# One chunk in twelve units gathered by SyncE with byte offsets, edge attributes issued by ScalarE, node updates inside the convolution's loop

## The reference, cut to what matters

```python
# attention: for each of three edge types t, over the edges of that type
xw = x @ W[t]; e = leaky_relu(a_s[src] + a_d[dst]); w = exp(e - max over dst)
out += segment_sum(w * xw[src]) / segment_sum(w) + bias[t]
# convolution
filters = silu(edge_attr @ fW1 + fb1) @ fW2 + fb2
messages = (x[src] @ dW + db) * filters
agg = segment_sum(messages, dst)
x + silu(agg @ uW1 + ub1) @ uW2 + ub2        # the node update
```

## Time and profile before

| | us |
|---|---|
| median of 3 runs | 4148.93 (4147.18 to 4151.31) |
| span of the profiled execution, which is its own time as far as it is given | 4155.8 |
| TensorE busy | 3395.1 |
| GpSimd busy | 3070.8 |
| VectorE busy | 2388.6 |
| ScalarE busy | 1364.7 |
| share of the 16 DMA engines: GpSimd's queue, SyncE's queue | 19.6%, 6.1% |

### The profile page before, as it was taken

One profiled execution on the slowest core, in us unless ns is written; L12 is line 12 of the kernel. 1 busy time (PEld: TensorE's weight loads), 2 busy tenths in 40 slices (PEclk: granted clock), 3 DMA queues, 4 the chain that ended last, 5 costly groups with the idle time before them and its releaser, 6 DMA issues.

```text
span 4155.8 us, 58597 instructions
## 1 busy us (share of the span) xinstructions
PE 3395.1 (82%) x13945; PEld 2624.2 (63%) x13946; DVE 2388.6 (57%) x5253; ACT 1364.7 (33%) x3361; POOL 3070.8 (74%) x3239
## 2 busy tenths in 40 slices
PE   5788788888888888888777888888888888788888
PEld 3566666666666666666555666666666666667666
DVE  7888888888888888888842322322332323223223
ACT  5455555555555555555411111111111111111111
POOL 5777777777777777777657777777777777777775
PEclk7555555555555555555577666676666666766667
DMA  4222222222222222222223222222222222222222
GB/s 124 56 59 61 59 59 61 60 59 61 59 59 61 59 59 61 59 59 61 58 60 98 77 74 76 71 76 75 71 76 73 74 75 72 75 76 71 76 74 79
DMA packets 180619, 286.01 MB, mean 69 GB/s; under 512 B 82273, under 2 KB 123054, under 8 KB 176011
## 3 DMA queue, kind: packets, MB, share of 16 engines
q0 software_dynamic: 102656, 213.73, 19.6%
q1 hardware_dynamic: 77856, 71.32, 6.1%
HBM read 271.06 MB, written 12.49 MB: 68 GB/s over the span
## 4 chain that ended last, share of the span: by engine, by line
POOL 36%; issue 12%; POOLq 1%; PE 1%; DMA 0%; DVE 0%; DVEq 0%
POOL ce_xg L63 36%; POOLq L676 0%; PE ce_ring L1429 0%; PE ce_ps_h L1420 0%; PE ce_ring L1420 0%; POOLq L677 0%; PE ce_ps_h L1407 0%; POOLq L688 0%; PE ce_ring L1385 0%; DMA ce_xg<-table,ce_idx 0%; POOLq L1275 0%; DVE ce_msg L1466 0%; POOLq L686 0%; DVE sums L1519 0%; DVEq L1275 0%
## 5 line engine op out<-in xcount | busy, mean ns | idle before, releaser
L63 POOL DMA_INDIRECT ce_xg<-table,ce_idx x1604 | 1520.8, 948 | 498.4 <-issue 488.9
L63 POOL DMA_INDIRECT ae_xg<-table,ae_idx x1604 | 1517.5, 946 | 501.8 <-issue 501.5
L1466 DVE TENSOR_TENSOR ce_msg<-ce_ring,ce_xg 128x768 f32<-128x768 f32 x269 | 257.7, 958 | 1333.7 <-DMA ce_xg<-table,ce_idx 1333.3
L924 PE MATMUL ae_ps_k<-ae_xg,ae_e 128*96 128x129 f32 x3224 | 882.4, 432 | 0.0
L1397 PE MATMUL ce_ps_h<-ce_ea,ce_fw 50*128 50x384 f32 x1076 | 611.9, 706 | 258.3 <-DMA ce_ea<-in_edge_attr 257.3
L1339 ACT ACTIVATE ce_hid<-ce_ps_h,ce_fb 128x768 f32<-128x768 f32 x269 | 242.5, 901 | 1749.6 <-PE ce_ps_h L1397 1749.6
L924 PEld LDWEIGHTS ae_ps_k<-ae_xg,ae_e 128*96 128x96 f32 x3224 | 689.4, 277 | 126.5 <-issue 117.1
L1376 PEld LDWEIGHTS ce_ring<-ce_fw,ce_hid 128*128 128x128 f32 x3228 | 582.2, 276 | 290.4 <-issue 151.8
L1376 PE MATMUL ce_ring<-ce_fw,ce_hid 128*128 128x128 f32 x3228 | 650.9, 376 | 65.5 <-DVE ce_msg L1466 65.4
L1385 PEld LDWEIGHTS ce_ring<-ce_hot,ce_msg 128*128 128x128 f32 x3224 | 521.1, 250 | 4.4 <-DVE ce_msg L1466 4.2
L1385 PE MATMUL ce_ring<-ce_hot,ce_msg 128*128 128x32 f32 x3224 | 507.3, 316 | 2.5 <-DVE sums L1474 2.5
(11 more groups left out here) (181 smaller groups left out, 3235.8 us busy)
## 6 DMA issues: line engine op xcount, KB each, us to landing
ce_ea<-in_edge_attr SPq DMA_DIRECT2D x90, 450.0 KB
ae_xg<-table,ae_idx POOLq DMA_INDIRECT x1604, 2.5
ce_xg<-table,ce_idx POOLq DMA_INDIRECT x1604, 2.5
ae_stage<-table SPq DMA_DIRECT2D x1024, 0.5 KB
ce_stage<-table SPq DMA_DIRECT2D x1024, 0.5 KB
sums<-in_x SPq DMA_DIRECT2D x7, 448.0 KB, 5.1
table<-sums SPq DMA_DIRECT2D x6, 462.0 KB, 3.6
pj_bias<-in_x_rows SPq DMA_DIRECT2D x42, 64.0 KB
```

The source lines that it names most:

```text
L63: eng.indirect_dma_start(out=out, out_offset=None, in_=table[:, :], in_offset=bass.IndirectOffsetOnAxis(ap=idx, axis=0)).then_inc(done, 16)
L924: last = nc.tensor.matmul(ps_k[0:KEYS, 0:D + 1], by_chunk[s % 3][:, c, :], xg[:, s % XS, c, 0:D + 1], start=(c == 0), stop=(c == count - 1))
L1466: nc.vector.tensor_tensor(msg[:, s % 3, :, :], filt, xg[:, s % XS, :, :], ALU.mult).then_inc(s_msg, 1)
```

## The change

In both phases a `Pace` with a span of 2 turns replaces `SPAN = 5`: 20 chunks are carried in each phase, 32 rows a half turn, read 16 at once. The list of all carried sources is loaded once per phase, and multiplied once by the bytes of a row (by GpSimd in `prepare`, by VectorE at the start of the convolution). The row DMA then has both sides as bytes, and its register is the offset. SyncE's wait for the landing of a delivery, and the attention's stores of a tile (`behind`), come after the 32 rows.

In the convolution ScalarE issues the attributes of the next turn, as soon as TensorE has read those of this one. And each turn from 2 to 43 updates one tile of nodes: first product on TensorE, Silu on ScalarE in slot 1, second product in slot 3, two additions on VectorE, store by SyncE one turn later. After the loop seven tiles are left, in two parts of 4 and 3. The attention's order on TensorE, VectorE and ScalarE stays as it was.

```diff
-SPAN = 5
-CARRIED = SPANS - 1
+READ = 16
+ATTENTION, CONVOLUTION = Pace(2, 20), Pace(2, 20)

     def collect(self, nc, sp, t, b, q):
-        todo = range(q * P // (SPAN * LOADS), (q + 1) * P // (SPAN * LOADS))
-        for first in range(todo[0], todo[-1] + 1, 8):
+        for first in range(q * share, (q + 1) * share, READ):
...
-            for p, row in zip(part, rows):
-                sp.dma_start(self.stage[p:p + 1, b, :], table[bass.ds(row, 1), :]).then_inc(self.rows_in, 16)
+            for p, start in enumerate(starts, first):
+                sp.dma_start(self.stage[p:p + 1, b, :].bitcast(u8), self.bytes[:, bass.ds(start, size)]).then_inc(self.rows_in, 16)

     def span(r, t, b, first=False):
...
-            following(r, SPAN * t + j, v)
-            if q == 0:
-                if not first:
-                    deliver(r, t, b)
-                sp.wait_ge(carry.list_in, 16 * (r * CARRIED + t + 1))
-                carry.read_list(sp, a, t + 2, b)
-                if not first:
-                    sp.wait_ge(carry.carried, 16 * (r * CARRIED + t))
-                    sp.sem_inc(carry.turn, 1)
-            carry.collect(nc, sp, table, 1 - b, q)
+            following(r, span_turns * t + j, v)
+            if q == 0 and not first:
+                deliver(r, t, b)
+            carry.collect(nc, sp, t, 1 - b, q)
+            if v == 0:
+                behind(r, span_turns * t + j)
+            if q == 0 and not first:
+                sp.wait_ge(carry.carried, 16 * (r * carried_chunks + t))
+                sp.sem_inc(carry.turn, 1)

 # prepare, GpSimd
+            pool.wait_ge(lists_in, 16)
+            nc.gpsimd.tensor_scalar(row_starts(state), row_starts(state), 4.0 * ROW, None, ALU.mult)

 # convolution, SyncE
+            def beside(r, i):
+                if closes(i):
+                    sp.wait_ge(t_y, r * DONE + i - OPEN)
+                    sp.dma_start(out[bass.ds((i - OPEN - 1) * P, P), :], done[:, :]).then_inc(out_done, 16)

 # convolution, ScalarE
                         act.wait_ge(s_hid, n + XS)
+                        if s % LOAD == LOAD - 1 and not (isinstance(i, int) and i == TURNS - 1):
+                            following_attributes(i, s // LOAD)
...
+                        if opens(i) and s == 1:
+                            act.wait_ge(t_u, k + 1)
...
+                            nc.scalar.activation(one_hid[:, :], tile_u, ACT.Silu, bias=update.b1[:, :]).then_inc(t_hid, 1)

 # convolution, TensorE
+                    if i is not None and opens(i) and s == UPDATE_SLOT:
+                        pe.wait_ge(t_hid, r * DONE + i - OPEN + 1)
+                        nc.tensor.matmul(tile_y, one_hid[:, :], update.w2[:, :], start=True, stop=True).then_inc(t_v, 1)
...
+                        if opens(i) and s == 1:
+                            pe.wait_ge(s_acc, r * UNITS + i * SL - 4)
+                            nc.tensor.matmul(tile_u, update.w1[:, :], acc[:, bass.ds((i - OPEN) * P, P)], start=True, stop=True).then_inc(t_u, 1)
...
+            for a0, a1 in HALVES:
+                nc.tensor.matmul(ps_u[:, a0 * P:a1 * P], update.w1[:, :], acc[:, (LAST + a0) * P:(LAST + a1) * P], start=True, stop=True).then_inc(s_u, 1)

 # convolution, VectorE
+            dve.wait_ge(lists_in, 16)
+            nc.vector.tensor_scalar(lists[:, :], lists[:, :], 4.0 * D, None, ALU.mult).then_inc(scaled, 1)
...
+                def update_tile(i):
+                    k = r * DONE + i - OPEN
...
+                        dve.wait_ge(out_done, 16 * k)
+                    nc.vector.tensor_tensor(done[:, :].unsqueeze(1), by_tile[:, bass.ds(i - OPEN, 1), :], update.b2[:, :].unsqueeze(1), ALU.add).then_inc(t_bias, 1)
+                    dve.wait_ge(t_v, k + 1)
+                    dve.wait_ge(t_bias, k + 1)
+                    nc.vector.tensor_tensor(done[:, :], done[:, :], tile_y, ALU.add).then_inc(t_y, 1)
```

More of the change, by code:

```diff
@@ L648, in load_indices @@
         span(r, 0, 0, True)
-        with sp.Fori(0, CARRIED // 2 - 1) as p:
+        span(r, 1, 1)
+        with sp.Fori(1, carried_chunks // 2) as p:
+            span(r, 2 * p, 0)
             span(r, 2 * p + 1, 1)
-            span(r, 2 * p + 2, 0)
-        span(r, CARRIED - 1, 1)
-        for q in range((SPAN - 1) * LOADS):
+        for q in range((TURNS - 1 - span_turns * carried_chunks) * LOADS):
             j, v = divmod(q, LOADS)
-            following(r, SPAN * CARRIED + j, v)
+            following(r, span_turns * carried_chunks + j, v)
+            if v == 0:
+                behind(r, span_turns * carried_chunks + j)
             if q == 0:
-                deliver(r, CARRIED, 0)
+                deliver(r, carried_chunks, 0)
+        sp.wait_ge(carry.carried, 16 * (r + 1) * carried_chunks)
+        sp.sem_inc(carry.turn, 1)
         for v in range(LOADS):
@@ L661, in load_indices @@
         beside(r, TURNS - 1)
+        behind(r, TURNS - 1)
     for v in range(LOADS):
         sp.wait_ge(idx_in[v], 16 * (passes * TURNS + 1))
-    sp.wait_ge(carry.list_in, 16 * (passes * CARRIED + 1))
     sp.sem_inc(landed, 1)
 def gather_units(pool, passes, table, xg, width, idx, idx_in, gathered, xg_free, pool_turn, carry):
+    span_turns, carried_chunks = carry.pace.span, carry.pace.carried
     with pool.Fori(0, passes) as r:
@@ L772, in beside, with behind @@
                     sp.dma_start(p.x[:, :], a["x_rows"][bass.ds((i - OPEN) * P, P), :]).then_inc(x_in, 16)
+            def behind(r, i):
                 if closes(i):
@@ L779, in _ @@
             sp.sem_inc(stored, 32)
-            load_indices(nc, sp, a, h, idx, idx_in, gathered, landed, carry, table, xg, s_sum, beside=beside)
+            load_indices(nc, sp, a, h, idx, idx_in, gathered, landed, carry, xg, s_sum, beside=beside, behind=behind)
             passes = pass_count(sp, h)
@@ new lines, in attributes @@
+                if isinstance(i, int) and i == 1:
+                    for g in range(v * (GROUPS - 1) // LOADS, (v + 1) * (GROUPS - 1) // LOADS):
+                        sp.dma_start(y[:, g, :, :], sent[g * GN:(g + 1) * GN, :].rearrange("(t p) f -> p t f", p=P)).then_inc(y_in, 16)
+            load_indices(nc, sp, a, h, sources.idx, sources.idx_in, gathered, sem_landed, carry, xg, s_msg, attributes, beside=beside, listed=lambda: sp.wait_ge(scaled, 1))
+            sp.wait_ge(out_done, 16 * DONE * pass_count(sp, h))
@@ L1399, in turn @@
                         if not (first and s < 1):
-                            filters(n - 1, (s - 1) % SL, first and s < 3)
+                            filters(n - 1, (s - 1) % SL, first and s < 3, i if s else None)
                         if not (first and s < 3):
                             sums(n - 3, (s - 3) % SL, first and s < 5)
-                turns(pe, turn)
+                finishing_turns(pe, turn)
                 n = (r + 1) * UNITS
@@ L1579 @@
     arrays["src"] = np.pad(src.reshape(NU // LOAD, 2, P // 2, LOAD * CH), ((0, 0), (0, 0), (0, 1), (0, 0)))
-    carried = (SPAN * SL * np.arange(1, SPANS) + CARRY_SLOT) * CH + CH - 1
-    arrays["src_rows"] = padded(given["src"], EP, 0).reshape(NU * CH, P)[np.append(carried, carried[0])]
+    rows = padded(given["src"], EP, 0).reshape(NU * CH, P)
+    arrays["src_rows"], arrays["messages_rows"] = (rows[pace.chunks].reshape(1, -1) for pace in (ATTENTION, CONVOLUTION))
     arrays["dst"] = by_unit(given["dst"], N).transpose(1, 0, 2)
```

232 lines of the change are left out of this document (108 added, 124 removed).

## The result

The changed kernel takes 4100.48 us (median of 4 runs, 4098.72 to 4101.96), the one before in runs beside it 4150.12: a ratio of 0.9876 [0.9862, 0.989], 1.2% faster. The prediction said 4101. The profiled execution lasts 4100.35 us with a span of 4098.5.

A forecast was written before the change was run, and what follows sets the result against it. The bound was taken to be the number of GpSimd's gathers times 1.25 us in both phases. Savings of 15.0 + 15.0 + 18.1 = 48.1 us from the runs' median of 4148.93 gave 4101 us, range 4092 to 4122.

The forecast's parts named there:

- Twelve gathers fewer at 1.25 us (15.0 + 15.0): GpSimd's gathers at L63: 12 fewer in each phase, saving 15.0 us in the attention and 15.0 in the convolution.
- The pace holds beside 2.5 times the rows: GpSimd's gathers in both phases: SyncE's additional row transfers don't slow their issue; cost 0, bounds -3.5 and +7 us.
- SyncE needs 60.5 of 88.8 us: SyncE's work in two turns of the attention: 60.5 us, at most 78.1, fits in 88.8, so indices come in time.
- the rival: SyncE's row bursts: byte rows issued dearly, over 0.56 us a row, make SyncE the bound; 4661 us, chance 0.05.
- Lateness of a delivery, stores behind the rows: 0.: SyncE's deliveries, and the attention's tile stores up to 18 us later, still come before they are needed; cost 0.
- TensorE's waits for attributes go, GpSimd waits for none of the convolution's edits: Convolution: 258 us of TensorE's waits go, four matmul records a turn add 63; cost 0, bounds 0 and +3.
- Scaling the lists: 0.: GpSimd's scaling, 7.2 us at most, fits in 12.9 idle; VectorE's in the convolution delays no needed message; cost 0.
- Tail 26.8 to 8.7: From last merge to end: only seven tiles left, 18.1 us saved, or 15 with TensorE at its lower clock.
- VectorE's slack in the attention, 137 us: VectorE's waits for gathers in the attention, 152.0 us before, shrink to about 137 and still cover the 15 saved.
- the rival in which it binds: VectorE's chain in the attention can't go faster, so the attention's 15.0 us stay: 4116 us, chance 0.06.
- the 48.1 of the sum: Total saving: 15.0 and 15.0 us from the two phases' gathers plus 18.1 from the tail.

The follow-up runs named there:

- the slow chip: A chip where the kernel before took 5428 us in place of 4150; the changed kernel, unaltered, took 5427.0 us there, ratio 0.999.
- row_numbers: Against the changed kernel: lists hold row numbers, not byte offsets, unscaled, with a register operation between fp32 rows; 4103.08 us, ratio 0.9874 to before.
- both edits undone: Against the changed kernel: row numbers with a register operation a row, and attributes issued by SyncE; 4104.54 us, or 6367.6 us where before took 5417.7.

## Why the prediction was right

- **Twelve gathers fewer at 1.25 us (15.0 + 15.0):** measured 18.8 and 15.4. The count is exact. The attention's other 3.8 are pace, 1.2510 to 1.2487 us, and the pace is no property of the kernel. The same changed program had a median of 1.249 us in its first trace and 1.252 in the one on the slow chip, and the kernel before 1.252 and then 1.249. The prediction had put 0 for the pace, with a bound of 3.5 us to this side. The convolution gained by its pace as well, but 3.2 us went back in a single gather (below).
- **The pace holds beside 2.5 times the rows:** right. The windows after and the run with half the rows show no cost. (The rule of the Trainium skill that the prediction weighed, "DMA: Bandwidth & Descriptors", Issuing engines are not separate DMA queues, is of transfers; the pace of issuing doesn't feel it here.)
- **SyncE needs 60.5 of 88.8 us:** four half turns with rows take it 62.5 in the attention and 63.2 in the convolution. The rows are 42 of it (43.5 said), the loads 10 (10.6 said), and all the rest is 10 to 11 us where the sum had 6.4. A row's period within a burst is 0.321 us in the median (0.34 said), a load of 16 took 1.145 and 1.208 (1.33 said). The split of a byte row into pieces that the rival weighed did not happen: SyncE's queue moved 83160 packets here and 83160 with rows of floats (`row_numbers`). The price of the rival was a threshold at 0.56 us a row, loads apart; with its loads that is 0.64. Counted from the first load to the last row, a burst of 32 took 0.41 to 0.43 us a row after, 0.51 with both edits undone (no loss) and 0.74 with loads of two (loss). The time that SyncE has free puts the threshold at 0.61 to 0.63, close to where the prediction had it.
- **Lateness of a delivery, stores behind the rows: 0.** No engine of the changed kernel waits for a delivery; right.
- **TensorE's waits for attributes go, GpSimd waits for none of the convolution's edits:** right, with 3.3 us in 11 waits for messages. The four records a turn cost 29.8 + 26.3 = 56 us where 63 were said. VectorE's wait for the tile's store, which the prediction named as a risk, came (77.8 us) and costs nothing: at 307.9 us it cost nothing either.
- **Scaling the lists: 0.** GpSimd's takes 6.7 us (7.2 said). Whether it delays the first gather isn't shown: that starts at 61.0 and 61.5 us in two kernels without it and from 61.3 on in those with it. VectorE's 0 was wrong, though by little: one gather of the convolution takes 4.15 us, 3.2 more than the others, by a mechanism that the prediction didn't have (below). How much of it reaches the total isn't clear: the convolution's gathers take 1992.5 and 1993.0 us in the two kernels without the scaling, 1993.4 to 1996.6 in the four with it in which GpSimd is the bound and SyncE carries twenty chunks.
- **Tail 26.8 to 8.7:** 7.5, and undoing it alone cost 21 us by the ratios and 19.3 by the trace. Of the 1.2 us that the prediction has too much nearly all lies behind the last addition, 4.1 us said and 2.9 measured. The clock did not fall there: 0.93 of full speed was granted in the last 7.5 us, and the products took 1.77 and 1.83 us, not twice what they did before.
- **VectorE's slack in the attention, 137 us:** 126. It gave 26 us where the gathers came 18.8 faster, and has five times as much left; the rival in which it binds falls.
- **Not foreseen:** 3.9 us between the phases, 3.0 of them by the shorter DRAIN of GpSimd.

The size came out within 1 us partly by luck. 3.9 us gained between the phases and 1.1 in the tail stand against 3.2 lost in one gather and 0.5 at the start. From trace to trace the change is 57.3 us and not the 48.1 of the sum, of which the pace makes up some 7.5: in the terms of the profiled execution the forecast was 4107.7, and the span is 4098.5. The forecast that hit is the one in terms of the medians, and how far a few runs even out the levels of the pace isn't shown. (The 6.9 us between trace and median compare a span with times; the changed kernel's profiled execution took 1.9 us more than its span, so for before 8.7 is the better estimate.) The mechanism does not rest on this: the runs show the gathers, the tail and the covered parts one by one.

## What to carry to other kernels

Ask first whose instruction count the time is. Here each gather taken from the engine that issues them is worth its 1.25 us, and waits of the other engines (258 us, 308 us) are worth nothing, however long their list: taking one away only renames it. But a helper that does the bound engine's work has an edge, and it is steep: with 3 us of 22 free nothing was lost, with 4 us too much work 13% of the kernel. Measure such a reserve over the stretches in which the helper has its work, since an average with the others (7.8 us here, not 6.5) hides how near the edge is. Edits that only give a helper reserve show no gain where all is well; on the slow chip the kernel without them was 17% slower.

## What was not expected of the hardware

**A small operation on VectorE holds up a gather.** GpSimd and VectorE of the changed kernel at the start of the convolution:

```profile
2095.73 4.15 POOL L63 DMA_INDIRECT ce_xg<-table,ce_idx  x1 [0.30 <-issue]
2097.65 1.42 DVE L1477 TENSOR_SCALAR ce_lists<-ce_lists 1x2560 int32<-1x2560 int32 x1
```

and with half the list:

```profile
2113.33 2.25 POOL L63 DMA_INDIRECT ce_xg<-table,ce_idx  x1 [0.30 <-issue]
2114.02 0.75 DVE L1477 TENSOR_SCALAR ce_lists<-ce_lists 1x1280 int32<-1x1280 int32 x1
```

The gather beside the scaling takes 3.2 us and 1.3 us longer than the usual 0.94. The stall has a fixed end: in all nine traces with the scaling that gather ends 0.81 to 0.82 us after it. Its length depends on when the gather began. On the slow chip (changed kernel) the gather that began 1.9 us ahead of the scaling ran through in 0.94 us and the next one took 2.91; in the trace above the one that began 1.9 us ahead is the one held up. That is 1 us more than a gather takes, so by the profile it should have been over before the scaling began; why it wasn't is open. Without the scaling (row numbers) the longest of the convolution is 1.125 us:

```profile
L63 POOL DMA_INDIRECT ce_xg<-table,ce_idx x1592: 940/944/1125, 2091.9 to 4084.8; - x199
```

A memset of 5.31 us on VectorE just ahead of it leaves the three gathers inside it at 0.94 to 0.98 us. The Trainium skill ("SBUF — State Buffer", SBUF: two separate sides) says that VectorE in a two-port mode and GpSimd lock a shared pair of ports against each other for a whole instruction. The stall agrees in direction. Whether the scaling ran in such a mode no trace shows, and that it holds up a gather that had begun before it, and to 0.8 us after it, the rule doesn't say.

**A register load of sixteen values costs less than one of five.** 430 ns for one value, 639 for two, 1145 for sixteen, each with about 0.15 us beside it. The lists of before, read 4 to 8 values at a time, took 554 to 2195. By the number of rows that follow each, the median is 0.57 us for four values, 1.33 for five and 1.94 for eight: sixteen at once cost less than five did. What makes five and eight so dear isn't shown.

**The pace of GpSimd's gathers has levels by execution**, 1.249, 1.250 or 1.252 us from one to the next as the median of a trace, for one and the same program: over 3200 gathers up to 10 us, as much as small changes to this kernel are worth. In the first pair of traces before has a mean of 946 ns in the attention and the changed kernel 944. In the second pair, both on the slow chip, it is the other way round: 944 before (the line is in the part on that chip), and after

```profile
L63 POOL DMA_INDIRECT ae_xg<-table,ae_idx x1592 | 1507.4, 947 | 1141.6 <-issue 495.7
```
